# New hand-written work lists for two attention layers: alternating heads, mixed widths, and row-maximum jobs 59 ahead

## The chip, the cores and the metric

One Trainium2 chip, one of its cores, one launch. The metric is the device time of the launch in microseconds (us). Three runs of the kernel before took 1375.84, 1375.1 and 1373.46 us; their median, 1375.1 us, is the time before. Engines: PE is TensorE (matmuls), PEld its weight loads, DVE is VectorE, ACT is ScalarE, POOL is GpSimd, SP issues the DMAs.

## The reference

Two transformer layers follow each other on x of shape (4, 1024, 128), float32. Each is attention over 16 heads of 8 elements and then a gated feed-forward with 384 hidden columns; the second attention is causal. All biases and the normalisation before each part are kept.

```python
x = x + attn_a(layernorm(x))      # 16 heads of 8, softmax(q k^T / sqrt(8)) v, full
x = x + ffn(layernorm(x))         # down(silu(gate(x)) * up(x)), int weights dequantised
x = x + attn_b(layernorm(x))      # the same with a mask: key position > query position is -inf
x = x + ffn(layernorm(x))
```

## The kernel before

**Windows.** A layer's attention is 16 windows: 4 sequences times 4 groups of 4 heads. A window's queries are two halves (f = 0, 1) of 512 columns; qb counts the 128-query blocks of a half, c the four heads, kh the two halves of 512 keys. Heads 0 and 2 have their operands on partitions 0 to 63, heads 1 and 3 on 64 to 127 ("even" and "odd" heads below). In the array these are two different row groups.

**Six kinds of work, in one list.** `Plan.walk` is a list of items, and every engine runs through the same list and does its own part of each item. The string `order` gives the items of one turn (one window's worth), one letter each:

- `j`, a job: PE multiplies 128 queries by up to 512 keys (L1094) into a ring of PSUM banks (4 banks in the full layer, 3 in the causal one), and DVE takes the row maximum (L876, or L873 with the mask for a diagonal block, followed by a small read of the accumulator). 64 jobs a window in the full layer, all 512 wide; 48 in the causal one, 24 of them 512 wide (16 of these without a mask) and 8 each 384, 256 and 128 wide.
- `h`, `H`, a shift: POOL splits the negated maxima of half 0 of the next window (`h`) or half 1 of this one (`H`) into two bf16 parts (L530, L532), PE transposes them (L1144), ACT copies them (L663), and SP sends them into two rows of the query operand (L424), so that the scores come out already shifted.
- `s`, scores: PE multiplies keys by queries with the shift (L1126, one head of 512 columns in the full layer, a pair of heads in the causal one, there with four small mask matmuls at L1134 on diagonal blocks), ACT takes the exponential (L647).
- `p`, sums: PE multiplies the probabilities of four heads by v (L1160), all into bank 7.
- `N`, `n`, a norm: ACT has copied bank 7 out (L654), PE transposes it (L1022), ACT copies (L668), DVE inverts the denominators (L905), POOL scales (L540).

**Running ahead.** `jobs_ahead` says how many jobs are done before the first turn: 48 in the full layer and 44 in the causal one, that is one window less or nearly so. `sums_behind` is how many `p` items trail. PE waits at a job until DVE has emptied the bank that was used a ring ago (`ring_free`), and at scores until ACT has emptied its bank.

**Start and end.** The first 48 jobs of the full layer are done in pairs by another route (`two_pairs`, `run_pair`: PE L1071 and L1076, ACT L714, DVE L856). `SHIFT_PAIR` says before which pair the first shift's bank is awaited. 18 (PE) and 22 (DVE) jobs of the causal layer are done inside the feed-forward of the first layer (`causal_jobs`); the rest of those ahead follow once the last q and k parts are stored. SP loads a window's operands (14 DMAs, 1 MB, L387 and L390) at the `H` of the window two before; for the first two windows before the shifts.

## Time and profile before

| | |
|---|---|
| median of 3 runs | 1375.1 us (1373.46 to 1375.84) |
| profiled execution, first to last instruction | 1375.5 us |
| full layer, 14 windows in steady state (101.4 to 677.7) | 576.3 us, 41.2 us each |
| causal layer, 13 windows in steady state (909.9 to 1273.2) | 363.3 us, 27.9 us each |
| busy: PE, DVE, ACT | 1322.9, 1180.3, 1009.6 us |

The profiled span is 0.4 us above the median and inside the range of the three runs, so differences worked out from the trace can be set against the median directly. In the timeline a row is a run of equal instructions on one engine: start, duration, engine, line, operation, and in square brackets the idle time before it and what ended it. A `L1160 ... x8` row is one `p` item (four heads, two passes each). A busy PE is not PE at its peak: matmuls overlap in the records, and the start-to-start distances say more than the durations.

### The profile page before, as it was taken

What the parts mean: (1) busy time and instruction counts of PE and PEld (TensorE: products, weight loads), DVE (VectorE), ACT (ScalarE), POOL (GpSimd) and SP (SyncE); (2) the same over time, 40 slices, a digit from 0 to 9 for tenths busy, and PEclk for the clock granted to TensorE, in tenths of its full rate; (3) what the DMA queues carried; (4) which work ended last, traced back from release to release, by engine and by line L of the source; (5) the groups of instructions that cost most, each with busy time, mean ns of one, the idle gap of its engine ahead of it and who ended that gap; (6) DMA issues with size and microseconds to landing.
All of it is one profiled execution on the core that took longest, in us unless ns stands there. A gap on an engine that the chain in (4) does not pass through costs nothing.

```text
span 1375.5 us, 26857 instructions
## 1 busy us (share of the span) xinstructions
PE 1322.9 (96%) x9681; PEld 679.7 (49%) x9681; DVE 1180.3 (86%) x2979; ACT 1009.6 (73%) x1791; POOL 142.5 (10%) x309
## 2 busy tenths in 40 slices
PE   9899999999999999999988987999999999999898
PEld 6444444444444444444435764555555555555487
DVE  7799999999999999999935987788888888888376
ACT  8678888888888888888883542677677776777743
POOL 5620000000000000000001211200000000000011
PEclk9699999999999999999998997899999999999999
DMA  7611101111101111101000333121112211120001
GB/s 212 189 32 32 30 4 32 32 32 33 28 7 32 33 33 32 30 6 31 2 1 1 110 106 93 33 59 38 34 33 49 48 33 34 41 56 3 3 24 39
DMA packets 40060, 58.44 MB, mean 42 GB/s; under 512 B 7796, under 2 KB 19448, under 8 KB 39928
## 3 DMA queue, kind: packets, MB, share of 16 engines
q1 hardware_dynamic: 39928, 56.72, 17.1%
q8 instruction: 77, 1.26, 0.4%
q14 instruction: 55, 0.45, 0.1%
HBM read 36.77 MB, written 18.87 MB: 40 GB/s over the span
## 4 chain that ended last, share of the span: by engine, by line
PE 84%; DVE 6%; ACT 5%; issue 3%; POOL 1%; DMA 1%; SPq 0%; DVEq 0%; POOLq 0%; ACTq 0%
PE psum L1160 28%; PE psum L1094 24%; PE psum L1126 16%; ACT probs L647 4%; PE psum L1022 3%; PE psum L1247 3%; PE psum L1231 2%; DVE maxima L876 2%; PE psum L1134 2%; PE psum L1176 1%; PE psum L1033 1%; DVE hid L952 1%; PE psum L1071 1%; PE psum L1007 1%; DVE junk L873 1%
## 5 line engine op out<-in xcount | busy, mean ns | idle before, releaser
L647 ACT ACTIVATE probs<-psum 128x512 f32<-128x512 f32 (+3 forms) x1386 | 832.3, 666 | 218.2 <-PE psum L1126 113.5
L876 DVE TENSOR_REDUCE maxima<-psum 128x1 f32<-128x512 f32 x1232 | 773.6, 682 | 33.3 <-PE psum L1094 27.8
L1094 PE MATMUL psum<-kop,qop 62*128 62x512 f32 (+3 forms) x1744 | 562.3, 437 | 7.5 <-DVE maxima L873 1.9
L1126 PE MATMUL psum<-qop,kop 64*128 64x512 f32 (+3 forms) x1792 | 522.0, 423 | 12.8 <-ACT probs L647 5.5
L1094 PEld LDWEIGHTS psum<-kop,qop 62*128 62x128 f32 x1744 | 267.2, 188 | 378.1 <-DVE maxima L876 285.6
L1160 PE MATMUL psum<-probs,v 128*32 128x512 f32 (+3 forms) x3584 | 441.9, 565 | 0.7 <-ACT probs L647 0.5
L1126 PEld LDWEIGHTS psum<-qop,kop 64*128 64x128 f32 x1792 | 266.8, 188 | 82.6 <-ACT probs L647 45.1
L873 DVE CUSTOM_DVE_ANT_0 junk<-psum,mask 128x384 bf16<-128x384 f32 (+3 forms) x512 | 232.2, 485 | 53.0 <-PE psum L1094 51.0
L1160 PEld LDWEIGHTS psum<-probs,v 128*32 128x32 f32 x3584 | 71.1, 109 | 100.8 <-issue 69.8
L1134 PE MATMUL psum<-half_ident,key_mask 64*128 64x64 bf16 x1024 | 88.8, 197 | 0.0
L540 POOL TENSOR_TENSOR att<-att_raw,rden 128x128 f32<-128x128 f32 x64 | 26.1, 407 | 512.5 <-DVE rden L905 512.5
L530 POOL TENSOR_TENSOR shift<-negmax,zeros 128x16 bf16<-128x16 f32 x64 | 14.1, 221 | 550.1 <-DVE negmax L882 542.1
L1231 PE MATMUL psum<-ffn_xt,gate_up_w 128*128 128x512 f32 x192 | 53.9, 417 | 5.5 <-DVE hid L952 5.3
L1134 PEld LDWEIGHTS psum<-half_ident,key_mask 64*128 64x128 bf16 x1024 | 49.0, 96 | 17.9 <-issue 8.6
L1247 PE MATMUL psum<-down_w,hid 128*128 128x128 f32 x384 | 47.6, 280 | 4.9 <-DVE hid L952 4.9
L739 ACT ACTIVATE hid<-psum 128x512 f32<-128x512 f32 x48 | 28.5, 597 | 31.7 <-PE psum L1231 31.4
L905 DVE RECIPROCAL rden<-att_raw 128x16 f32<-128x16 f32 x64 | 15.7, 245 | 39.2 <-ACT att_raw L668 39.2
L1247 PEld LDWEIGHTS psum<-down_w,hid 128*128 128x128 f32 x384 | 45.0, 194 | 7.5 <-DVE hid L952 7.2
L1022 PE MATMUL psum<-ident,sums 128*128 128x128 f32 x256 | 41.1, 283 | 5.0 <-ACT sums L654 1.6
L787 DVE TENSOR_TENSOR x<-psum,x 128x512 f32<-128x512 f32 x32 | 22.1, 690 | 26.1 <-PE psum L1247 13.6
L614 ACT ACTIVATE qk<-psum,bqk 128x512 f32<-128x512 f32 x32 | 21.1, 682 | 30.2 <-PE psum L1033 30.1
L873 DVE DVE_READ_ACCUMULATOR2_ANT maxima<- 128x1 f32 x512 | 42.7, 83 | 0.1
(102 smaller groups left out, 751.6 us busy)
## 6 DMA issues: line engine op xcount, KB each, us to landing
qop<-q_parts SPq DMA_DIRECT2D x256, 64.0 KB
kop<-k_parts SPq DMA_DIRECT2D x64, 128.0 KB
kop<-k_parts SPq DMA_DIRECT2D x128, 64.0 KB
q_parts<-parts SPq DMA_DIRECT2D x24, 256.0 KB, 2.9
k_parts<-parts SPq DMA_DIRECT2D x24, 256.0 KB, 3.1
x<-in_L_attn_a_x SPq DMA_DIRECT2D x8, 256.0 KB, 4.0
q_parts<-att SPq DMA_DIRECT2D x8, 256.0 KB, 3.6
k_parts<-att SPq DMA_DIRECT2D x8, 256.0 KB, 3.6
```

The source lines that it names most:

```text
L540: nc.gpsimd.tensor_tensor(dst, att_raw[:, f, :, :, 0:HD], rden[:, f].rearrange("p t (h o) -> p t h o", o=1).broadcast_to([P, TPC, HG, HD]) ...
L647: nc.scalar.activation(probs[:, slot, heads[0] % 2:heads[-1] % 2 + 1, c0:], psum[:, bank:bank + len(heads), c0:], ACT.Exp, scale=SCORE_SCA ...
L739: nc.scalar.activation(hid[:, c, :], psum[:, 2 + 2 * (c % 2), :], ACT.Silu, scale=DEQUANT).then_inc(silu_ready, 1)
L873: nc.vector.tensor_tensor_reduce(out=junk[:, slot, 0:width], in0=src, in1=mask[:, CHUNK - width:], scale=1.0, scalar=LOWEST, op0=ALU.add, ...
L876: nc.vector.tensor_reduce(dst, src, AX_X, ALU.max).then_inc(ring_free, 1)
L1022: ins = nc.tensor.transpose(psum[:, bank, t * P:(t + 1) * P], src[:, t, :], ident[:])
L1094: mm(psum[:, bank, 0:width], qop[rows, buf, f, r, qb * P:(qb + 1) * P].bitcast(F32R), kop[rows, buf, r, kh * CHUNK:kh * CHUNK + width].bit ...
L1126: ins = mm(psum[:, bank + k, c0:], kop[rows, buf, c // 2, j * P:(j + 1) * P].bitcast(F32R), qop[rows, buf, f, c // 2, c0:].bitcast(F32R), ...
L1134: ins = mm(psum[:, bank + k, at:at + TILE_ROWS], key_mask[rows, part, :], half_ident[rows], start=False, stop=part == 1)
L1160: ins = mm(psum[32 * c:32 * c + 32, 7, c0:], v[:, at:at + 32], probs[:, slot, c % 2, c0:], start=(j == 0), stop=(s == plan.half_end[f]), t ...
L1231: ins = mm(psum[:, 2 + 2 * (c % 2) + k, :], gate_up_w[:, k, c, :].bitcast(F32R), ffn_xt[:, part].bitcast(F32R), start=part == 0, stop=part ...
L1247: ins = mm(psum[:, 7, t * P:(t + 1) * P], hid[:, c, t * P:(t + 1) * P], down_w[:, c, :], start=(c == 0), stop=(c == FB - 1))
```

## The change

Both `order` strings are replaced. The full layer's stream of jobs now alternates between an even and an odd head (`alternate=True`; the causal one did before), so the pairs of the opening stretch are numbered differently (`run_pair`) and `SHIFT_PAIR` is worked out instead of written (it becomes 22, was 20). The causal layer starts 59 jobs ahead instead of 44, which makes the walk begin one turn earlier, and its jobs come in a written list, one token `c qb kh` for each, in place of the loop's order of rising widths. All jobs, scores, sums, norms and shifts are the same ones in the same number.

```diff
@@ Plan.__init__
+        if tiles:
+            found = {x[:4]: x for x in stream}
+            stream = [found.pop((f, *(int(d) for d in token))) for f in range(2) for token in tiles[f].split()]
+            assert not found
+        self.first_job = stream[0]
@@
-        for turn in range(-1, WINDOWS + 1):
+        for turn in range(-2, WINDOWS + 1):
@@ PLANS
-PLANS = [Plan(causal=False, heads=HEAD_UNITS, unit_ring=3, job_ring=4, alternate=False,
-              order="jsjjsspjssjsjpjsjsjnsjjssp...",
+PLANS = [Plan(causal=False, heads=HEAD_UNITS, unit_ring=3, job_ring=4, alternate=True,
+              order="sjjsjpsjjjsspsjjsjspsjjsjs...",
               jobs_ahead=48, sums_behind=2, project_at=(9, 11, 14), wide_step=5),
          Plan(causal=True, heads=PAIR_UNITS, unit_ring=2, job_ring=3, alternate=True,
-              order="sjjsjpjsjsjpjjjHsjjsjpjsjjspjjsjsjsjjnjjspj...",
-              jobs_ahead=44, sums_behind=1, project_at=(4, 6, 10))]
+              order="jjHjsjjsjjjspjssjjpjsjjsjspjjssjjpsjjpjssjj...",
+              jobs_ahead=59, sums_behind=1, project_at=(4, 6, 10),
+              tiles=("120 110 030 130 020 320 330 100 230 010 220 300 000 310 210 200",
+                     "310 121 311 100 030 300 211 200 321 031 201 230 110 ..."))]
-SHIFT_PAIR = 20
+SHIFT_PAIR = 2 * -(-[item[0] for item in PLANS[0].walk].index("shift") // 4)
@@ run_pair's number; the wait for a window's operands
-                        run_pair(plan, f, c, qb, number // 2)
+                        run_pair(plan, f, c, qb, number // 4 * 2 + c % 2)
-                if (f, c, qb, kh) == (0, 0, 0, 0):
+                if job == plan.first_job:
```

Three places show how instructions move. Lines are 6 higher in the kernel after from here on (L1094 is L1100, L1126 is L1132, L1160 is L1166, L1022 is L1028, L1144 is L1150).

PE in the full layer, around the norm of half 0 of the second window (L1160 sums, L1094 jobs, L1126 scores, L1022 the norm's transposes), before:

```order
L1160 MATMUL psum<-probs,v 32x512 x4
L1094 MATMUL psum<-kop,qop 128x512
L1126 MATMUL psum<-qop,kop 128x512
L1094 MATMUL psum<-kop,qop 128x512
L1126 MATMUL psum<-qop,kop 128x512
L1094 MATMUL psum<-kop,qop 128x512
L1022 MATMUL psum<-ident,sums 128x128 x4
L1126 MATMUL psum<-qop,kop 128x512
L1094 MATMUL psum<-kop,qop 128x512 x2
```

and now, the same norm, followed by the shift of the next window:

```order
L1132 MATMUL psum<-qop,kop 128x512
L1028 MATMUL psum<-ident,sums 128x128 x4
L1150 MATMUL psum<-ident_bf,shift 32x128
L1100 MATMUL psum<-kop,qop 128x512 x2
L1132 MATMUL psum<-qop,kop 128x512
L1100 MATMUL psum<-kop,qop 128x512
L1132 MATMUL psum<-qop,kop 128x512 x2
L1166 MATMUL psum<-probs,v 32x512 x4
L1132 MATMUL psum<-qop,kop 128x512 x2
L1100 MATMUL psum<-kop,qop 128x512 x3
```

The norm stood three jobs behind the last `p` of its half; four more `p` items now lie between, and the shift `h` follows it at once, with 6 jobs from there to the scores that use it (11 before).

PE at the start of the causal layer, from the first shift (L1144) to the first scores (L1126), before:

```order
L1144 MATMUL psum<-ident_bf,shift 32x128
L1094 MATMUL psum<-kop,qop 128x512 x2
L1094 MATMUL psum<-kop,qop 128x384 x2
L1094 MATMUL psum<-kop,qop 128x512 x4
L1126 MATMUL psum<-qop,kop 128x512 x2
```

and now, with both shifts of the first window ahead of its scores:

```order
L1150 MATMUL psum<-ident_bf,shift 32x128
L1100 MATMUL psum<-kop,qop 128x384 x2
L1100 MATMUL psum<-kop,qop 128x512
L1100 MATMUL psum<-kop,qop 128x128
L1100 MATMUL psum<-kop,qop 128x512
L1100 MATMUL psum<-kop,qop 128x256
L1100 MATMUL psum<-kop,qop 128x384
L1100 MATMUL psum<-kop,qop 128x128 x2
L1150 MATMUL psum<-ident_bf,shift 32x128
L1100 MATMUL psum<-kop,qop 128x256
L1132 MATMUL psum<-qop,kop 128x512 x2
```

44 jobs stood ahead of the first scores, 62 do now; the first shift is transposed after job 52 (was 36), the second after job 61.

PE in the causal layer's steady state, around its two norms, now (before they stood apart, 17 jobs from each other; L1140 is the mask):

```order
L1166 MATMUL psum<-probs,v 32x512 x4
L1100 MATMUL psum<-kop,qop 128x256
L1100 MATMUL psum<-kop,qop 128x512 x2
L1150 MATMUL psum<-ident_bf,shift 32x128
L1028 MATMUL psum<-ident,sums 128x128 x8
L1100 MATMUL psum<-kop,qop 128x384 x2
L1132 MATMUL psum<-qop,kop 128x256 x2
L1140 MATMUL psum<-half_ident,key_mask 128x64 x4
L1100 MATMUL psum<-kop,qop 128x512
L1166 MATMUL psum<-probs,v 32x384 x4
```

A shift and both norms now stand in one block, and jobs of 256, 512 and 384 columns stand next to each other.

## Rows read from the trace of the kernel before

**Rows 1.** The page, part 1: busy us, share of the span, instructions.
```profile
PE 1322.9 (96%) x9681; PEld 679.7 (49%) x9681; DVE 1180.3 (86%) x2979; ACT 1009.6 (73%) x1791; POOL 142.5 (10%) x309
```
**Rows 2.** Busy us by stretch: length, PE, PEld, DVE, ACT, POOL, then granted clock.
```profile
101.40:677.70 576.30, 572.30 (x3726) 241.92 (x3725) 560.69 (x953) 485.60 (x981) 23.12 (x84) 1.00 0.12 26
852.10:873.70 21.60, 21.16 (x128) 11.78 (x128) 13.06 (x49) 11.99 (x16) 9.74 (x5) 0.51 0.23 50
909.90:1273.20 363.30, 359.62 (x3460) 190.19 (x3462) 315.22 (x1092) 264.14 (x391) 21.43 (x78) 1.00 0.18 37
```
**Rows 3.** Who waited for whom, 101.4 to 677.7 us: total, times, longest.
```profile
PEld psum L1094 <- DVE maxima L876: 209.7, 308, 0.8
...
DVE maxima L876 <- PE psum L1094: 10.5, 28, 0.4
```
**Rows 4.** Timeline of a full-layer window: PE between two sums.
```profile
304.04 1.07 PE L1160 MATMUL psum<-probs,v 128*32 128x512 f32 x8
305.04 0.49 PE L1094 MATMUL psum<-kop,qop 62*128 62x512 f32 x1
...
305.94 0.64 PE L1160 MATMUL psum<-probs,v 128*32 128x512 f32 x4
```
**Rows 5.** The same window: DVE's jobs, and PE and DVE around its norm.
```profile
304.34 15.12 DVE L876 TENSOR_REDUCE maxima<-psum 128x1 f32<-128x512 f32 x24
...
318.07 0.42 PEld L1022 LDWEIGHTS psum<-ident,sums 128*128 128x128 f32 x4 [0.51 <-issue]
...
321.13 0.69 DVE L876 TENSOR_REDUCE maxima<-psum 128x1 f32<-128x512 f32 x1 [0.38 <-PE psum L1094]
```
**Rows 6.** PE at the last shift and the scores that need it.
```profile
1282.29 0.22 PE L1144 MATMUL psum<-ident_bf,shift 128*32 128x128 bf16 x1 [0.17 <-POOL shift L532]
...
1285.43 0.78 PE L1126 MATMUL psum<-qop,kop 64*128 64x512 f32 x4 [0.28 <-DMA qop<-shift_rows]
```
**Rows 7.** Who waited for whom, 909.9 to 1273.2 us.
```profile
DVE junk L873 <- PE psum L1094: 38.6, 103, 0.7
...
DVE maxima L876 <- PE psum L1094: 7.6, 13, 0.6
```
**Rows 8.** DVE in a causal window: masked jobs of 512 and 128 columns.
```profile
1056.26 0.68 DVE L873 CUSTOM_DVE_ANT_0 junk<-psum,mask 128x512 bf16<-128x512 f32 x1
...
1056.87 0.69 DVE L873 CUSTOM_DVE_ANT_0 junk<-psum,mask 128x512 bf16<-128x512 f32 x1
...
1058.80 0.29 DVE L873 CUSTOM_DVE_ANT_0 junk<-psum,mask 128x128 bf16<-128x128 f32 x1 [0.72 <-PE psum L1094]
```
**Rows 9.** Causal layer: sums on PE, exponentials of two heads on ACT.
```profile
1033.72 0.64 PE L1160 MATMUL psum<-probs,v 128*32 128x256 f32 x8
...
1035.10 2.85 ACT L647 ACTIVATE probs<-psum 128x1024 f32<-128x1024 f32 x3 [0.26 <-PE psum L1126]
...
1038.52 0.85 PE L1160 MATMUL psum<-probs,v 128*32 128x384 f32 x8
...
1040.43 1.06 PE L1160 MATMUL psum<-probs,v 128*32 128x512 f32 x8
...
1042.60 1.07 PE L1160 MATMUL psum<-probs,v 128*32 128x512 f32 x8
```
**Rows 10.** The start of the causal layer.
```profile
847.08 1.38 SPq L424 DMA_DIRECT2D qop<-shift_rows  x2
...
848.65 0.69 DVE L873 CUSTOM_DVE_ANT_0 junk<-psum,mask 128x512 bf16<-128x512 f32 x1
...
852.08 0.79 PE L1126 MATMUL psum<-qop,kop 64*128 64x512 f32 x2 [3.71 <-DMA qop<-shift_rows]
...
853.63 1.29 DVE L876 TENSOR_REDUCE maxima<-psum 128x1 f32<-128x512 f32 x2 [4.29 <-PE psum L1094]
```
**Rows 11.** PE at the first scores of the second and of the last causal window.
```profile
886.68 0.48 PE L1126 MATMUL psum<-qop,kop 64*128 64x512 f32 x2
...
1277.76 0.48 PE L1126 MATMUL psum<-qop,kop 64*128 64x512 f32 x2
```

More of the change, by code:

```diff
@@ L51, with __init__ @@
 class Plan:
-    def __init__(self, causal, heads, unit_ring, job_ring, alternate, order, jobs_ahead, sums_behind, project_at, wide_step=99):
+    def __init__(self, causal, heads, unit_ring, job_ring, alternate, order, jobs_ahead, sums_behind, project_at, wide_step=99, tiles=None):
         self.causal, self.heads, self.unit_ring, self.job_ring = causal, heads, unit_ring, job_ring
@@ L82, in __init__ @@
                 width = (TPC * f + qb + 1) * P if causal else S
-                tiles = [(c, kh) for r in range(PAIRS) for kh in range(2) for c in (2 * r, 2 * r + 1)] if alternate \
+                in_head_order = [(c, kh) for r in range(PAIRS) for kh in range(2) for c in (2 * r, 2 * r + 1)] if alternate \
                     else [(c, kh) for c in range(HG) for kh in range(2)]
-                for c, kh in tiles:
+                for c, kh in in_head_order:
                     w = min(width - kh * CHUNK, CHUNK)
@@ L147 @@
 PAIR_UNITS, HEAD_UNITS = ((0, 1), (2, 3)), ((0,), (1,), (2,), (3,))
-PLANS = [Plan(causal=False, heads=HEAD_UNITS, unit_ring=3, job_ring=4, alternate=False,
-              order="jsjjsspjssjsjpjsjsjnsjjsspjssjsjpjsjsjsjjsspjssjsjpHjsjsjsjjsspjssjsjpjsjsjsjjsspjssjsjpjsjsjNsjjsspjssjsjpjsjsjsjjsspjssjsjphjsjsjsjjsspjssjsjpjsjs",
+PLANS = [Plan(causal=False, heads=HEAD_UNITS, unit_ring=3, job_ring=4, alternate=True,
+              order="sjjsjpsjjjsspsjjsjspsjjsjspsjsjsjjsjssjjsjspHssjjsjpsjjsjspjjsjsspjsjssjsjjsnjsjjsspjssjsjpjssjsjpjssjsjpsjjsjspsjjsjspsjjsjsjsjsjsNhjjsjsspssjjjsps",
               jobs_ahead=48, sums_behind=2, project_at=(9, 11, 14), wide_step=5),
          Plan(causal=True, heads=PAIR_UNITS, unit_ring=2, job_ring=3, alternate=True,
-              order="sjjsjpjsjsjpjjjHsjjsjpjsjjspjjsjsjsjjnjjspjsjsjjpjsjjsjpjjsjsjpjjsjNjjsphjjspjjjspjjspjs",
-              jobs_ahead=44, sums_behind=1, project_at=(4, 6, 10))]
-SHIFT_PAIR = 20
-assert [item[0] for item in PLANS[0].walk].index("shift") in range(2 * SHIFT_PAIR - 3, 2 * SHIFT_PAIR + 1)
+              order="jjHjsjjsjjjspjssjjpjsjjsjspjjssjjpsjjpjssjjpjsjjsjpsjjjspjjssjjpjjsjspjjjhnNjjsjpjjssjjp",
+              jobs_ahead=59, sums_behind=1, project_at=(4, 6, 10),
+              tiles=("120 110 030 130 020 320 330 100 230 010 220 300 000 310 210 200",
+                     "310 121 311 100 030 300 211 200 321 031 201 230 110 231 120 210 221 330 021 001 320 010 301 331 111 000 101 011 131 220 130 020"))]
+SHIFT_PAIR = 2 * -(-[item[0] for item in PLANS[0].walk].index("shift") // 4)
 PE_JOBS_AHEAD, DVE_JOBS_AHEAD = 18, 22
```

## The prediction

> **What bounds the kernel now.** The page comes first: PE is busy for 96% of the span and DVE for 86% [rows 1]. An average over unlike stages says little, so I split the span by stretches [rows 2]. In the 14 steady windows of the full layer DVE works 560.69 of 576.3 us: 15.6 us idle, 1.1 a window. In the 13 steady windows of the causal layer it works 315.22 of 363.3: 48.1 us idle, 3.7 a window. The waits say who keeps DVE idle: PE, for 10.5 us in 28 waits (two a window) in the full layer [rows 3] and 46.2 us in 116 waits in the causal one [rows 7]. PE waits for DVE as well, 209.7 us by its weight loads in the full layer [rows 3], much of it while the sums before still stream. The full layer is thus DVE's, with a small hole at each norm; the causal layer belongs to neither, PE and DVE take turns.
>
> That caps the gain. No list can take more than 1.1 us from a full window, as DVE's jobs stay the same: 24 of them take 15.12 us, 0.63 apiece [rows 5], and 64 x 0.63 is 40.3 of the window's 41.2.
>
> **The full layer's list: PE's share.** Rows 4 give PE's prices: sums begin at 304.04, the next work at 305.04, the next sums at 305.94. So sums cost 1.00, and the six matmuls between 0.90. At the granted clock of 1.00 [rows 2], 2.4 GHz, 512 columns take 0.213, so six in a row would be 1.28: some run side by side. An even and an odd head lie on different rows of the array. The six are (o odd, e even; j job, s scores) jo so se je so je; if only unequal parities overlap, that makes four turns (jo; so with se; je with so; je) of 0.225 each. Counted by the list, a window had 80 such turns; the new list has 64, the least possible for 128 matmuls in pairs. PE gets 16 x 0.225 = 3.6 us lighter a window. Before it had about 16 x 1.0 + 80 x 0.225 + 2 norms and 2 shifts (2) = 36 of 41.2 us, now 32.4.
>
> The Trainium skill ("TensorE: Matmul & The Clock Gate", Part 3, the mechanism) says that a weight load overlaps running matmuls only when its row group differs. By it the six matmuls need four turns, 0.85 us, and the trace's 0.90 agrees [rows 4]; with three turns, as if any two overlapped, they would need 0.64, and the new list would then save PE nothing.
>
> This work lies beside DVE's, so it buys only the holes. The hole: the norm's transposes come three jobs behind the last sums and need ACT's copy of them; PE's weight load stands idle 0.51 us until 318.07, and DVE idles 0.38 before its next job at 321.13 [rows 5]. Now four more sums lie between the last sum of a half and its norm, so that wait goes, at both norms: 28 waits, 10.5 us in 14 windows, 0.75 each. What comes new: stretches with four scores around one sum between two jobs (s s p s s): two turns and the sums, 0.45 + 1.00 us of PE, while a ring of four jobs feeds DVE for 2.5 us, less the 0.5 from a matmul's start to its reduce; and the shift H only 4 jobs behind the last job of its half, where POOL's result comes about 0.1 us after PE does. I let these cost 0.2. A window gains 0.53, 15 windows 8 us. Bounds: 0 and the whole idle time, 16.
>
> The shift h stands 6 jobs before the scores that need it, 11 before. From the transpose to the landing took 3.14 us in the one place where scores waited for it, 1282.29 to 1285.43 [rows 6]. Six jobs are 3.8 us, and seven scores lie there too. It fits with 0.6 to spare; I count nothing, and 0.5 a window if ACT is late with the copy. The first window's shift is 4 jobs later (job 42, was 38) with one pair of pairs behind it: +0.4. In the tail three sums instead of two stand behind the last scores: +0.5.
>
> **The causal layer: steady state.** I cut a window at its sums and add up for each stretch what each engine must do. Prices: DVE 0.61, 0.48, 0.35 and 0.22 for a masked job of 512, 384, 256, 128 columns (starts at 1056.26 and 1056.87; the durations 0.69 and 0.29 at 512 and 128 columns give 0.13 for each 128 [rows 8]), 0.63 unmasked; PE 1.00 for sums of 512 columns [rows 4] 0.225 a turn of 512, narrower in proportion, and as estimates 0.43 for sums of 128 (those between in line), 0.2 for a mask's four, 0.75 a norm, 0.3 a shift; ACT 0.95 for a pair of heads at 512 (2.85 for three [rows 9]), in proportion below. For example the stretch from 1033.72 to 1038.52 took 4.80 us [rows 9]: DVE 4.70, PE 3.2, ACT 4.0, so it was DVE's. The ones from 1038.52 and 1040.43 took 1.91 and 2.17: DVE 1.70 and 1.83, PE 1.8 and 1.9, so PE's or nobody's. Over twelve stretches the largest of the three sums to 26.8 before and 27.8 was measured; the new list sums to 26.9, its PE work to 24.7 (24.4 before) and DVE's to the same 24.0. PE's is larger since the written list puts three odd heads in a row (310 121 311): 47.4 turns, 45.9 before.
>
> So without carrying over, nothing is won. The lists differ in what can be carried: before one stretch has 1.5 us more DVE than PE work, and then eight have less, and behind sums the queue of three jobs often holds 128 or 256 columns, 0.2 to 0.4 us of cover against 1.0 of sums: there DVE idles, as 0.72 before 1058.80 [rows 8]. With mixed widths no stretch has more than 0.6 excess, which three queued jobs of mean 0.5 can carry. Of the 1.5 us of excesses I take a third as saved: 0.5 a window, 14 windows, 7 us. Bounds: 1.9 gained (half of DVE's idle time) and 0.8 lost (PE's 0.3 and 0.5 at the block of h and both norms, where PE is away from jobs for 0.3 + 2 x 0.75 = 1.8 us and the queue holds 1.2 to 1.5).
>
> **The causal layer: start and end.** DVE had its 44 jobs done at 849.3 and stood still until 853.63, since the first shift's DMA went out only at 847.08, behind the operands' 14, and landed at 852.08 [rows 10]. Now 59 jobs must be emptied before PE reaches the first scores. By the prices above jobs 0 to 58 are 28.8 us of DVE, jobs 0 to 43 were 21.0: 7.8 more; the first job of window 1 may wait 0.5 for its operands, which land just ahead of that 852.08. Scores begin at 857.8, 5.7 later. The 4.3 us hole is filled by that. Given back: the granted clock was 0.51, the 1.2 GHz level, from 852.1 to 873.7 [rows 2], and the turn from 852.08 to 886.68 took 34.6 instead of 27.9 [rows 10, 11]: 6.7 us over 21.6 at the low level; if the clock returns at the same moment, 5.7 of these pass without scores, -1.7. At the end turn 14 has 14 jobs fewer and PE's 23.4 bounds it, about 24.5: -3.4; the last turn from 1277.76 [rows 11] loses its 4 jobs: -0.5. Sum +0.1. In the feed-forward, the first nine causal jobs are wide now (4.45 us of DVE, was 2.76), of which 0.4 shows.
>
> Operands: load of window w+2 now waits for the last sums of w-1, 29 jobs or 16 us before their first use; The shift that queued behind such a load landed 5 us after its issue at 847.08 [rows 10]; with 0.6 for each of a load's 14 issues (an estimate from that row's 1.38 for two) a load is in after some 8.4 + 5 = 13 us. Hidden by 3; were it not, 1 us a window. SP has nothing else queued behind that wait but the next shift, 33 jobs later.
>
> **Sum.** -8.0 + 0.4 + 0.5 - 7.0 + 0.1 + 0.4 = -13.6. The profiled execution (span 1375.5) is 0.4 above the median of 1375.1, so the sum is set against the median: 1361.5 us.
>
> **Rivals.** (a) The mixed widths do more: DVE's idle time in the causal layer halves, 1.9 a window, 27 us; with the full layer's 8 it gives 1341. For it: 103 of its waits come from masked jobs [rows 7], which the list spreads. Against: PE's own work is 24.7 of 27.9. (b) Slower: the causal list makes PE the bound. Same-parity jobs (0.3) and the block h n N with two waiting inverses on DVE (0.5, or up to 1.2 together with idle DVE behind it) cost 1.2 x 14 = 17, the later start its 5.7 with 1.5 given back; with 8 gained in the full layer: 1375.1 + 17 + 4.2 - 8 = 1388 at worst, 1380 at 0.6 a window. It decides when PE's work per window passes what the balance saves, about 0.4 us. (c) Nothing changes: holes at the norms in the full layer reappear at the tight places (s s p s s, H four jobs behind), and the causal layer comes out even: 1374.5. For it: DVE is at 97% there already, and the two lists' stretch sums differ by 0.1.
>
> **Chances.** The forecast, 1350 to 1371: 0.50. (a) 0.15. (b) 0.22. (c) 0.13, of which 0.02 ends just beyond what can be told. A measurement of this kernel tells about 0.2%, 2.7 us, from no change. From these: faster 0.50 + 0.15 + 0.02 = 0.67, same 0.11, slower 0.22. The range reaches to (a) and into (b): 1341 to 1382; the forecast's own is 1350 to 1371.
>
> **What would show it.** Full layer: a window of 40.7, waits of DVE for PE under 4 us in 14 windows, PE's weight loads waiting longer for DVE than before; wrong if scores wait for the shift's DMA in each window. Causal layer: a steady window of 27.4, DVE idle near 3.2, fewer waits after narrow jobs; wrong with DVE idle above 4 or a window above 28. Start: the causal layer's first scores near 852.1 - 6.7 + 5.7 = 851, and no 4.3 us hole of DVE ahead of them. End: about 4 us shorter from the first scores of window 14. The forecast fails as a whole if the full layer is not faster, since its gain rests on the removed wait alone.

## The result and the profile after

The changed kernel took 1335.1 us (median of 4 runs, 1332.8 to 1338.3) against 1374.6 for the kernel before in the same comparison: ratio 0.972, 95% interval 0.970 to 0.974. That is 39.5 us less; 13.6 were forecast and the range ended at 1341. The profiled execution has a span of 1336.4 us (1375.5 before). Here and below medians and ranges take in every execution, while a ratio leaves out those that ran over 1.5% above the fastest of their kernel, which is so in one run, the causal order alone (two of its four).

By milestones of the two traces, in us:

| stretch | before | after | difference | predicted |
|---|---|---|---|---|
| to the first scores of the full layer | 64.7 | 66.2 | +1.6 | +0.4 |
| first to last scores, full layer | 662.2 | 637.8 | -24.3 | -8.0 |
| from there to the first causal job | 91.5 | 89.4 | -2.1 | +0.5 |
| to the first causal scores | 33.8 | 44.0 | +10.3 | +6.1 |
| first to last scores, causal layer | 455.6 | 432.1 | -23.5 | -12.6 |
| to the end | 67.8 | 66.9 | -0.9 | 0 |

The last column sorts the prediction's terms into these stretches; in the causal one it is -7.0, -1.7, -3.4 and -0.5.

Busy us by stretch of the changed kernel (length, PE, PE's weight loads, DVE, ACT, POOL, granted clock, then DMA): ten full windows, ten causal ones, and the causal turn 14.

```profile
199.73:594.23 394.50, 392.32 (x2662) 158.14 (x2663) 393.63 (x681) 347.46 (x701) 17.01 (x60) 1.00 0.14 29
951.09:1219.50 268.41, 268.16 (x2661) 144.88 (x2661) 246.36 (x841) 199.79 (x300) 16.16 (x60) 1.00 0.19 42
1219.50:1243.90 24.40, 24.28 (x255) 13.00 (x255) 19.57 (x62) 19.98 (x30) 1.61 (x6) 1.00 0.01 3
```

The same cut of the kernel before, ten windows each, so that windows can be compared one to one (they are in line with [rows 2]):

```profile
204.33:616.00 411.67, 408.83 (x2662) 172.79 (x2661) 400.51 (x681) 346.84 (x702) 16.51 (x60) 1.00 0.13 27
975.36:1254.90 279.54, 276.56 (x2662) 146.32 (x2662) 242.48 (x841) 203.18 (x300) 16.49 (x60) 1.00 0.19 40
```

A full window fell from 41.17 to 39.45 us, a causal one from 27.95 to 26.84. The first is the surprise: the prediction had called 40.3 the least that any list could reach. DVE's *busy* time fell as well, from 40.05 to 39.36 a window, with the very same 681 instructions in ten windows. It is idle for 0.09 us a window now, where it was for 1.12. So of the 1.72 us that a window lost, 1.03 came out of DVE's idle time and 0.69 out of its busy time. In the causal layer DVE's idle time went from 3.7 to 2.2 a window, while its busy time rose from 24.2 to 24.6.

Who waits for whom in the same ten full windows after. Against [rows 3] PE's wait for DVE before a job has shrunk, its wait for ACT before scores has taken over, and DVE's wait for PE is gone from the list (in ten windows before they were 149.8, 6.7 and 7.5 us):

```profile
PEld psum L1132 <- ACT probs L653: 105.5, 170, 0.8
PEld psum L1100 <- DVE maxima L882: 46.3, 70, 0.8
```

The start of the causal layer after, which answers to [rows 10]: DVE waits while PE projects, PE waits for window 1's operands, and the first scores come at 837.47, 44.0 us behind the first causal job.

```profile
811.54 0.89 DVE L804 TENSOR_TENSOR v<-psum,bvo 128x128 f32<-128x128 f32 x4 [2.40 <-PE psum L1041]
...
830.39 0.87 PE L1100 MATMUL psum<-kop,qop 62*128 62x384 f32 x3 [1.38 <-DMA kop<-k_parts]
...
831.24 0.56 DVE L879 CUSTOM_DVE_ANT_0 junk<-psum,mask 128x384 bf16<-128x384 f32 x1 [1.26 <-PE psum L1100]
...
837.47 1.00 PE L1132 MATMUL psum<-qop,kop 64*128 64x512 f32 x2
```

### The profile page after: what moved, and what is told of

Read it like the earlier page. It is cut to its first block, busy times and chain, and to the rows that moved or that the text cites. A ratio compares the mean times of both kernels' runs of the same rounds, so it can differ in the third digit from the quotient of the medians.

```text
span 1336.4 us, 26857 instructions
## 1 busy us (share of the span) xinstructions
PE 1290.7 (97%) x9681; PEld 656.2 (49%) x9681; DVE 1176.7 (88%) x2979; ACT 1004.5 (75%) x1791; POOL 142.1 (11%) x309
## 3 DMA queue, kind: packets, MB, share of 16 engines
q8 instruction: 77, 1.26, 0.4%
## 4 chain that ended last, share of the span: by engine, by line
PE 88%; DVE 5%; ACT 3%; issue 2%; DMA 1%; SPq 0%; POOL 0%; DVEq 0%; ACTq 0%; POOLq 0%
PE psum L1166 30%; PE psum L1132 21%; PE psum L1100 21%; PE psum L1253 4%; PE psum L1028 3%; PE psum L1237 2%; ACT probs L653 2%; PE psum L1140 2%; PE psum L1039 1%; DVE maxima L882 1%; DVE hid L958 1%; PE psum L1182 1%; PE psum L1077 1%; PE psum L1013 1%; PE psum L1150 1%
## 5 line engine op out<-in xcount | busy, mean ns | idle before, releaser
L653 ACT ACTIVATE probs<-psum 128x512 f32<-128x512 f32 (+3 forms) x1386 | 821.8, 669 | 153.0 <-PE psum L1132 83.0
L1100 PE MATMUL psum<-kop,qop 62*128 62x512 f32 (+2 forms) x1744 | 519.4, 429 | 7.0 <-DVE maxima L879 3.1
L1132 PE MATMUL psum<-qop,kop 64*128 64x512 f32 (+3 forms) x1792 | 514.2, 427 | 9.2 <-ACT probs L653 7.9
L1166 PE MATMUL psum<-probs,v 128*32 128x512 f32 (+3 forms) x3584 | 440.5, 564 | 0.7 <-ACT sums L660 0.7
L1100 PEld LDWEIGHTS psum<-kop,qop 62*128 62x128 f32 x1744 | 266.4, 189 | 203.4 <-DVE maxima L882 119.3
L1132 PEld LDWEIGHTS psum<-qop,kop 64*128 64x128 f32 x1792 | 247.5, 187 | 232.1 <-ACT probs L653 205.9
L879 DVE CUSTOM_DVE_ANT_0 junk<-psum,mask 128x512 bf16<-128x512 f32 (+3 forms) x512 | 232.6, 487 | 38.7 <-PE psum L1100 34.9
L1166 PEld LDWEIGHTS psum<-probs,v 128*32 128x32 f32 x3584 | 71.1, 108 | 120.0 <-issue 89.2
L1140 PE MATMUL psum<-half_ident,key_mask 64*128 64x64 bf16 x1024 | 74.3, 197 | 0.0
L669 ACT CAST shift_rows<-psum 32x128 f32<-32x128 bf16 x64 | 16.5, 258 | 56.2 <-PE psum L1150 56.2
L1140 PEld LDWEIGHTS psum<-half_ident,key_mask 64*128 64x128 bf16 x1024 | 43.2, 96 | 18.4 <-issue 6.5
L745 ACT ACTIVATE hid<-psum 128x512 f32<-128x512 f32 x48 | 28.5, 598 | 30.3 <-PE psum L1237 29.9
L620 ACT ACTIVATE qk<-psum,bqk 128x512 f32<-128x512 f32 x32 | 21.1, 684 | 32.8 <-PE psum L1039 32.6
L1028 PE MATMUL psum<-ident,sums 128*128 128x128 f32 x256 | 38.7, 283 | 2.4 <-ACT sums L660 1.6
```

The costliest lines, as they stand in the source:

```text
L653: nc.scalar.activation(probs[:, slot, heads[0] % 2:heads[-1] % 2 + 1, c0:], psum[:, bank:bank + len(heads), c0:], ACT.Exp, scale=SCORE_SCA ...
L745: nc.scalar.activation(hid[:, c, :], psum[:, 2 + 2 * (c % 2), :], ACT.Silu, scale=DEQUANT).then_inc(silu_ready, 1)
L879: nc.vector.tensor_tensor_reduce(out=junk[:, slot, 0:width], in0=src, in1=mask[:, CHUNK - width:], scale=1.0, scalar=LOWEST, op0=ALU.add, ...
L1028: ins = nc.tensor.transpose(psum[:, bank, t * P:(t + 1) * P], src[:, t, :], ident[:])
L1100: mm(psum[:, bank, 0:width], qop[rows, buf, f, r, qb * P:(qb + 1) * P].bitcast(F32R), kop[rows, buf, r, kh * CHUNK:kh * CHUNK + width].bit ...
L1132: ins = mm(psum[:, bank + k, c0:], kop[rows, buf, c // 2, j * P:(j + 1) * P].bitcast(F32R), qop[rows, buf, f, c // 2, c0:].bitcast(F32R), ...
```

## The experiments

"Window" is the mean of ten in the profiled execution, cut at ACT's copies of the shift. A run without a ratio is a single execution. The kernel before stood at 1374.9 to 1376.9 us in the comparisons with several rounds, at 1374.1 in the last.

### Which list gives what

The first run takes the new full list and leaves the causal layer as it was.

```diff
 # the changed kernel, but PLANS[1] as before
-order="jjHjsjjsjjjspjss...", jobs_ahead=59, ..., tiles=("120 110 ...", "310 121 ..."))]
+order="sjjsjpjsjsjpjjjH...", jobs_ahead=44, ...)]
```

> The full layer wholly new, the causal layer wholly old. If the two layers' gains add up: full window 39.4 as in the kernel after, causal window 27.9 as before, first causal scores 28.7 us behind the last addition of the first feed-forward's chunk as before, the whole at 1375 - 24 - 2 = 1349. If the causal lists are what shortens the start or the clock's stretches elsewhere, it lies outside 1345 to 1353.

Measured: 1352.4 us, ratio 0.983 (0.981 to 0.985). The full window is 39.45, the causal one 27.96. So the full list brings 23 us, and the causal one the other 17 (1352.4 to 1335.1): each layer's window is the same whichever list the other layer has, and both gains are larger than forecast.

### The two parts of the full list, one at a time

```diff
 # heads alone: the old order of letters, but
-Plan(..., alternate=False,
+Plan(..., alternate=True,
```

> The kernel before with only the heads of the full layer's jobs alternating; both orders, the 44 jobs ahead and the causal widths are the old ones. Theory A (the alternation of heads relieves PE: 80 turns of 512 columns become fewer, DVE's jobs are no longer a little late): a full window falls from 41.2 to about 39.8 us, the whole to about 1355. Theory B (the order of the letters does it, where the sums stand between jobs; parity is worth little): a full window stays within 0.3 of 41.2, the whole within 5 us of 1375.

```diff
 # order alone: alternate=False, but
-order="jsjjsspjssjsjpjsjsjnsjjssp...",
+order="sjjsjpsjjjsspsjjsjspsjjsjs...",
```

> The full layer gets the new order but its jobs keep the old sequence of heads (two halves of keys of one head after each other); the causal layer is the old one. Theory A (heads): a full window near 41, the whole near 1373. Theory B (order): a full window of 39.4 to 39.8, the whole about 1350. If it takes both, it lies above 41.2 here, as the order was drawn up for pairs that this kernel does not have.

Measured: heads alone 1417.2 us, ratio 1.031 (1.029 to 1.034), window 44.1. Order alone 1389.4, ratio 1.010 (1.008 to 1.012), window 41.9. Each part alone makes the kernel slower, by 41 and by 14 us; together they save 23. The two were written for each other: the order says which kinds of matmul are neighbours, the sequence of heads says which of these lie on different rows of the array.

PE with the heads alone, between two sums; this is the stretch of [rows 4], which had 0.90 us between the end of one sums' 1.00 and the start of the next:

```profile
309.56 0.50 PE L1098 MATMUL psum<-kop,qop 62*128 62x512 f32 x1
309.57 0.72 PE L1130 MATMUL psum<-qop,kop 64*128 64x512 f32 x2
309.91 0.40 PE L1098 MATMUL psum<-kop,qop 62*128 62x512 f32 x1
310.14 0.39 PE L1130 MATMUL psum<-qop,kop 64*128 64x512 f32 x1
310.37 0.40 PE L1098 MATMUL psum<-kop,qop 62*128 62x512 f32 x1
310.70 1.06 PE L1164 MATMUL psum<-probs,v 128*32 128x512 f32 x8
```

The six matmuls take 1.13 us instead of 0.90: the last score and the last job are both of odd heads now, and start 0.23 apart (310.14 and 310.37). In the kernel before they start together (310.68 and 310.69), and the next sums follow at 311.01:

```profile
310.10 0.49 PE L1094 MATMUL psum<-kop,qop 62*128 62x512 f32 x1
310.11 0.73 PE L1126 MATMUL psum<-qop,kop 64*128 64x512 f32 x2
310.45 0.40 PE L1094 MATMUL psum<-kop,qop 62*128 62x512 f32 x1
310.68 0.39 PE L1126 MATMUL psum<-qop,kop 64*128 64x512 f32 x1
310.69 0.39 PE L1094 MATMUL psum<-kop,qop 62*128 62x512 f32 x1
```

DVE with the heads alone: three jobs, and then it waits for PE.

```profile
310.10 1.89 DVE L880 TENSOR_REDUCE maxima<-psum 128x1 f32<-128x512 f32 x3 [0.25 <-PE psum L1098]
312.23 1.89 DVE L880 TENSOR_REDUCE maxima<-psum 128x1 f32<-128x512 f32 x3 [0.24 <-PE psum L1098]
```

### Where the rest of the full window went

The traces of before and after differ in something that no row calls a wait. A fed DVE starts its jobs of 512 columns 0.600 to 0.610 us apart, while one lasts 0.68 in the records: it overlaps the next by 0.08. A job that starts less than 0.08 late shows no idle time. In the kernel before, 44 of the 60 distances a window between neighbouring jobs are at most 0.61, but some 14 are 0.63 to 0.74 (the other two are the holes at the norms); after, 52 are at most 0.61, and 8 are 0.63 to 0.73. Four runs ask who makes them late.

```diff
 # lighter sums, odd key blocks only (their results are left out but for 64 columns; 1.0 is added)
-mm(psum[..., c0:], v[...], probs[..., c0:], ...)
+mm(psum[..., c0:end], v[...], probs[..., c0:end], ...)     # end = c0 + 64 if j % 2 == 1
```

> The kernel before with PE made lighter: the sums of odd key blocks cover 64 columns instead of up to 512 (these sums are left out beyond that, and 1.0 is added to every sum to keep the denominators away from zero). DVE's jobs are untouched. Theory: DVE's jobs cost 0.605 from start to start and not the 0.63 of the prediction; the rest was lateness of PE of under 0.1 a job that shows as no idle time because a job's recorded end overlaps the next start. Then a full window falls from 41.2 to 39.4, and mean start-to-start distances from 0.638 to about 0.608. Rival: 0.63 is DVE's own pace in that list (PSUM banks shared with ACT and PE): the full window stays at 40.5 or more. In the causal layer a window of 24.5 to 26 would say that PE bounds it, 27 or more that it does not.

Measured: 1359.6 us, window 40.30, between the theory's 39.4 and the rival's 40.5. Nearly the whole of the lateness is gone but for four distances a window at the norms, and PE is idle for 1.9 us a window where it was idle for 0.3.

```diff
 # the last job of each long stretch one score later, 8 times a window
-...jjssp...
+...jsjsp...
```

> The kernel before; in its full layer the last job of every long stretch goes one score later, next to the sums (jsjjssp becomes jsjsjsp, 8 times a window), nothing else. In the trace of before about 13 of 64 jobs a window start 0.07 to 0.13 us late on DVE without any idle time that the rows show. Theory 1, they are late because two scores and the sums lie between two jobs there: the distance between those jobs falls by a score's 0.23, the lateness goes, the window falls from 41.2 to about 40.3 us, the time by 13. Theory 2, the place of the sums is set by ACT, which frees the scores' three banks, and the job only moves within the same time: the window stays at 41.1 to 41.3.

Measured: 1372.0 us, window 41.31. Theory 2. The place of that job is free: what moved is only which matmul waits. PE's scores waited for ACT 40 times in ten windows before (6.7 us), and in this run, ten windows:

```profile
PEld psum L1126 <- ACT probs L647: 38.5, 160, 0.4
```

```diff
 # both norms two sums later, at the same place of the next long stretch
-...jsjsjnsjjssp...      ...jsjsjNsjjssp...
+...jsjsjsjjssp (jssjsj p) jsjsjnsjjssp...
```

> The kernel before with both norms of the full layer two sums later, at the same place of the next long stretch (after the third of its five jobs), nothing else. The prediction's theory, a norm's hole comes from its wait for ACT's copy of the last sums: that wait goes, 0.5 to 0.75 us a window, 40.5 us and 8 to 10 us of the time. Rival, the hole is the 0.75 us of transposes themselves, in a stretch where PE has no time to spare, wherever they stand: 41.1 to 41.4.

Measured: 1375.6 us, window 41.34. Moving the norm away from the last sums of its half, which the prediction called the gain of the new list, brings nothing: DVE still waits for PE twice a window (7.8 us in 25 waits between 125 and 640 us, 9.3 in 25 before).

```diff
 # ACT: exponentials of odd key blocks over 256 of 512 columns, full layer
-nc.scalar.activation(probs[..., c0:], psum[..., c0:], ACT.Exp, ...)
+nc.scalar.activation(probs[..., c0:end], psum[..., c0:end], ACT.Exp, ...)     # end = 256
```

> The kernel before, but in the full layer ACT's exponentials of odd key blocks cover only 256 of 512 columns (the rest of those blocks is left as it was): 32 of 64 a window are 0.2 us shorter, 6.8 us of ACT's 34 a window; PE's and DVE's work stays. Theory A, in the old list the five scores between two jobs' sums wait for ACT to free the three banks, and that sets when the sums and the next jobs come: the window falls from 41.2 to 40.0 to 40.6 us. Theory B, PE and DVE alone set it: 41.1 to 41.2.

Measured: 1352.2 us, window 39.70, more than theory A had asked for. With the old list, and neither PE's nor DVE's work touched, 1.5 of the 1.7 us are there. DVE still waits for PE twice a window, 4.1 us in ten.

So the old window was set by a circle that has no DVE in it. The rows of the kernel before, ACT's exponentials, PE's scores (L1126) and its sums (L1160):

```profile
307.54 2.56 ACT L647 ACTIVATE probs<-psum 128x512 f32<-128x512 f32 x5
308.59 0.58 PE L1126 MATMUL psum<-qop,kop 64*128 64x512 f32 x2
309.11 1.07 PE L1160 MATMUL psum<-probs,v 128*32 128x512 f32 x8
310.11 0.73 PE L1126 MATMUL psum<-qop,kop 64*128 64x512 f32 x2
310.87 0.60 ACT L647 ACTIVATE probs<-psum 128x512 f32<-128x512 f32 x1 [0.77 <-PE psum L1126]
...
311.01 1.07 PE L1160 MATMUL psum<-probs,v 128*32 128x512 f32 x8
312.01 0.50 PE L1126 MATMUL psum<-qop,kop 64*128 64x512 f32 x1
```

Follow it round. The scores have a ring of three banks, so the fifth score of a long stretch needs the end of its second exponential. ACT begins the five at 307.54 and is at the end of the second some 1.1 us later; the fifth score starts just then (the second of the two in the row at 308.59). The sums stand behind it, 309.11; the next scores behind the sums, 310.11; ACT has been idle for 0.77 by then. Then the short stretch, sums at 311.01, the first score of the next long stretch at 312.01, its exponential 0.57 later: 312.58, that is 5.04 us after 307.54. DVE needs 8 x 0.605 = 4.84 for the eight jobs of this time. From sums to sums, the eight rounds of a window take 5.03 four times, 5.07 twice (with a shift) and 5.46 twice (with a norm's transposes), which is the window's 41.2. With the shorter exponentials the round of 5.03 takes 4.84, DVE's own time. Each of the four runs fits: a shorter exponential or shorter sums shorten the circle, a moved job or norm does not.

After, PE and ACT go in even steps of 1.90 for thirteen of a window's sixteen sums, mostly three scores and three jobs between two sums:

```profile
302.86 1.06 PE L1166 MATMUL psum<-probs,v 128*32 128x512 f32 x8
...
304.75 1.07 PE L1166 MATMUL psum<-probs,v 128*32 128x512 f32 x8
...
306.65 0.64 PE L1166 MATMUL psum<-probs,v 128*32 128x512 f32 x4
```

The scores that are left over stand in three long stretches of eight or nine (4.6, 4.8 and 5.4 us between their sums). In a step of 1.90 PE works all the time, 1.00 + 0.90, and DVE needs 3 x 0.605 = 1.82 for its three jobs: this is where some are a little late still.

The same relief of PE on the changed kernel shows what is left:

```diff
 # the changed kernel with the lighter sums of the first run of this section
```

> The changed kernel with the weighted sums of odd key blocks cut to 64 columns, as in the run on the kernel before (a stand-in is added so that nothing divides by zero): some 0.8 us less of PE at every second sums. Theory 1, the full layer is DVE's now, and its queue never runs dry: the full window stays at 39.4 us, 0.9 below what the old list reached with the same relief (40.3). Causal layer: if PE ends last there, its window falls from 26.8 to 26.0 or less, if DVE and ACT, it stays above 26.5. Theory 2, PE still sets the full window: 38.9 or less.

Measured: 1334.1 us in all, hardly less than the changed kernel's 1335.1, as the clock was low in one full and two steady causal windows (0.87, 0.74 and 0.88 granted; the two causal ones took 32.6 and 29.3 us). The full window is 38.77, most of the other causal windows 26.5. Ten full windows:

```profile
197.97:585.69 387.72, 382.46 (x2662) 172.61 (x2662) 387.71 (x681) 344.94 (x700) 16.90 (x60) 1.00 0.14 29
```

Neither theory: it is between them. DVE is busy for 387.71 of 387.72, its jobs 0.598 apart. This is DVE's real floor, 38.8; the changed kernel is 0.7 above it, in the eight late starts a window that no row calls a wait.

### The two parts of the causal list

```diff
 # order alone: the changed kernel without the written widths
-              tiles=("120 110 030 130 ...", "310 121 311 100 ..."))]
+              tiles=None)]
```

> The changed kernel, but the causal layer takes its jobs in the loop's sequence of widths; its new order of letters and the 59 jobs ahead stay. Counted by the list, PE's jobs and scores between two sums need 41.5 turns a window (the larger count of even or odd heads in each stretch), against 45.8 in the changed kernel and 42.0 before. Theory W, the mixed widths carry the causal gain: the window goes back to 27.9 us and the time to 1350 us. Theory O, the order of letters carries it: the window stays at 26.9 and the time at 1335, a little lower for the lighter PE. Theory P, order and widths are written for each other, as order and heads were in the full layer: the window is above 28.3 and the time above 1356.

```diff
 # widths alone: the changed kernel with the old causal order and 44 ahead
-order="jjHjsjjsjjjspjss...", jobs_ahead=59,
+order="sjjsjpjsjsjpjjjH...", jobs_ahead=44,
```

> The changed kernel, but the causal layer has its old order of letters and 44 jobs ahead; only the written list of widths is new there. 46.2 turns a window. Theory W: the window is 26.9 us and, with the old start, the time 1333 to 1338. Theory O: the window goes back to 27.9 and the time to 1350 or more. Theory P: the window is above 28.3 and the time above 1356.

Measured: 1403.6 us (1380 to 1410), ratio 1.010 (1.002 to 1.018), and 1402.0 (1392 to 1406), ratio 1.020 (1.018 to 1.023). Theory P. With the order alone, two causal windows at the full clock and one with a low clock:

```profile
1055.90:1084.80 28.90, 28.38 (x271) 14.26 (x267) 24.67 (x85) 20.48 (x30) 1.59 (x7) 1.00 0.18 39
1187.00:1216.00 29.00, 28.46 (x274) 14.45 (x266) 24.78 (x85) 20.52 (x31) 1.66 (x8) 1.00 0.19 39
...
1247.40:1281.50 34.10, 33.58 (x268) 17.06 (x268) 24.93 (x85) 20.82 (x30) 1.61 (x6) 0.80 0.16 33
```

With the widths alone, one of each:

```profile
1010.30:1040.20 29.90, 28.67 (x268) 14.93 (x268) 24.62 (x84) 20.24 (x30) 1.65 (x6) 1.00 0.18 37
1040.20:1073.90 33.70, 32.66 (x268) 16.98 (x270) 24.86 (x84) 20.74 (x31) 1.65 (x6) 0.85 0.15 34
```

At the full clock a window is 28.9 with the order alone and 29.9 with the widths alone; both lists old give 27.96, both new 26.84. It is the picture of the full layer again: each part spoils what the other half was tuned to. On top, the granted clock fell to the 1.2 GHz level inside steady causal windows, in more than half of them for the order alone and in three for the widths alone (in the profiled executions, of 1408 and 1392 us); such a window costs another 4 to 5 us. So the windows bear Theory P out, while the times hold the clock's share too: 0.9 and 2.0 us a window over the old causal list are some 13 and 28 us in fourteen windows (an estimate), of the 51 and 50 us that these runs took over the one with that list. PE was idle for 0.5 and 1.2 us of a window at the full clock there, for 0.3 in the kernel before and 0.03 in the changed one.

### Even and odd heads in the causal list

```diff
 # 16 of 48 tokens, only the head (first digit) changes, widths stay; the first ones:
-"120 110 030 130 020 320 330 100 230 010 220 300 000 310 210 200"
+"120 110 230 030 020 320 330 100 130 010 220 000 300 210 310 200"
```

> The changed kernel with the same widths in the same places of the causal list; only which head a job is of is exchanged between jobs of equal width, at 16 of 48 places, so that in each stretch between sums even and odd heads are near equal: 42.25 turns a window instead of 45.75, that is 3.5 x 0.225 = 0.8 us less of PE's work. DVE's and ACT's work stays as it is, in length and order. Theory 1, PE ends last in a causal window: 0.4 to 0.8 a window less, 14 windows: 1324 to 1330 us. Theory 2, DVE and ACT bound the window, DVE with 2.2 us of idle time that the scores' waits for ACT leave: nothing within 3 us of 1335.

Measured: 1344.6 us, ratio 0.978 (0.976 to 0.979), window 27.32: 0.5 slower than the changed kernel, against both theories. Stretch by stretch, the three whose count fell most, by 0.75 to 1 turn, kept their time within 0.08 us (2.74 and 2.73, 2.03 and 2.05, 3.25 and 3.33), and two got longer. One of them in the changed kernel, its last two jobs and the next sums:

```profile
1064.47 0.42 PE L1166 MATMUL psum<-probs,v 128*32 128x128 f32 x8
...
1065.83 0.40 PE L1100 MATMUL psum<-kop,qop 62*128 62x512 f32 x2
1066.16 0.42 PE L1166 MATMUL psum<-probs,v 128*32 128x256 f32 x4
```

and with the exchanged heads:

```profile
1068.35 0.42 PE L1166 MATMUL psum<-probs,v 128*32 128x128 f32 x8
...
1069.76 0.64 PE L1100 MATMUL psum<-kop,qop 62*128 62x512 f32 x2
1070.32 0.42 PE L1166 MATMUL psum<-probs,v 128*32 128x256 f32 x4
```

An even and an odd job start together (the pair lasts 0.40) and the sums follow 0.33 behind; two odd ones start one behind the other (0.64) and the sums follow after 0.56. The stretch grew from 1.69 to 1.97, the other one, with two even jobs at its end, from 1.52 to 1.73: together the 0.5.

```diff
 # 6 of 48 tokens; the two stretches above as in the changed kernel
-"... 020 320 330 100 230 010 220 300 000 310 210 200", "310 121 311 100 030 300 211 200 ..."
+"... 020 220 330 100 230 310 320 300 000 010 210 200", "310 121 211 100 030 300 311 200 ..."
```

> The changed kernel with heads exchanged at six of 48 places of the causal list, between jobs of equal width: 42.75 turns a window by the same count as in the run with balanced heads, 45.75 in the changed kernel. That run's list made two stretches longer, by 0.2 and 0.3 us, where its two last jobs before the sums came to be of one parity; these two stretches are kept here as in the changed kernel. Theory 1, only the last matmuls ahead of the sums count, those that follow PE's last wait in the stretch, and turns saved elsewhere lie beside PE's waits for DVE and ACT: the window stays at 26.8 us and the time within 3 us of 1335. Theory 2, turns count wherever they lie: 42.75 turns give 26.1 us and 1325. Theory 3, what made the other list slower was something else, as the 16 exchanges: 27.1 or more, 1340.

Measured: 1334.7 us, ratio 0.970 (0.967 to 0.973), window 26.88. Theory 1. A count of 42.75 turns and one of 45.75 take the same time; what tells is the pair that stands last before the sums. It is also not clearly better than the changed kernel (0.972, 0.970 to 0.974), so no version here beats it.

### Does the causal layer wait for ACT?

```diff
 # causal layer: exponentials of every second step over the first half of their columns
+end = (c0 + CHUNK) // 2 if plan.causal and s % 2 == 1 else CHUNK
```

> The kernel before, but in the causal layer ACT's exponentials of every second step cover only the first half of their columns (the rest is left as it was, and a stand-in is added to the sums so that nothing divides by zero): 12 of 24 a window are shorter, by 1.9 us of ACT's 20.3 in all. PE's and DVE's work stays. Theory A, the old causal list is held by scores that wait for ACT, as the old full list was: its window falls from 27.9 to 27.3 us or less. Theory B, it is held by PE's and DVE's turns: 27.7 to 27.9.

> The same relief on the changed kernel. Theory A: if the new list still waits for ACT, its window falls from 26.8 to 26.4 us or less; if the new list has taken ACT out of what bounds the window, it stays at 26.7 to 26.8. Theory B: 26.7 to 26.8 with the old list unchanged as well.

Measured: 1376.2 us with the old lists, window 28.03; 1334.7 with the new ones, window 26.77. ACT's busy time fell by 3 us a window in both (2.9 and 2.8; 1.9 were expected) and nothing followed. So ACT does not hold the causal window, in either list. Theory B's other half, that PE's and DVE's turns do, is not shown: the lighter sums, which shorten PE's, moved the causal windows by 0.4 in the old list (27.54, where 27 or more was to say that PE does not bound it) and by 0.3 in the new one (26.5). What holds a causal window, and what in the new list gives the 1.11, no run isolates. What the traces show is that DVE's waits for PE before masked jobs fell from 80 to 50 in ten windows, and those before unmasked ones (5.9 us in 10 waits) are gone. The first row is of the ten windows before, the second of the ten after:

```profile
DVE junk L873 <- PE psum L1094: 30.4, 80, 0.7
...
DVE junk L879 <- PE psum L1100: 18.9, 50, 0.8
```

## Why the prediction was wrong

Faster was right; the size was not. One of the signs to look for in the full layer came, DVE's waits for PE are gone. Another came out the other way: PE's weight loads were to wait longer for DVE, and they wait for 46.3 us in ten windows instead of 149.8. And moving the norms, the reason given for the full layer's gain, brings nothing by itself; that this layer got faster all the same was luck. Point by point:

**"The full layer is thus DVE's, with a small hole at each norm"; "no list can take more than 1.1 us from a full window".** This is the step that failed. It rests on 24 jobs in 15.12 us, 0.63 apiece [rows 5]. But 0.63 was not a price. The 24 hold late starts, up to 0.08 us of each hidden as busy time by the records' overlap; fed, a job costs 0.605, and with nothing in the way 0.598. The floor was 38.8, not 40.3, and the list took 1.72 of 41.17, not 0.53: 1.03 of idle time, nearly all that the prediction allowed for, and 0.69 of busy time, which it took as fixed. From the first to the last scores that is 24.3 us, of which 8 were forecast. The bound at the other end, 16, was too low for the same reason.

**"So it buys only the holes"; the norm's wait.** The waits of DVE for PE did vanish [rows 3], as predicted, but they were a result and not the cause: with the norms moved away in the old list, nothing is gained. The cause was the circle of ACT's exponentials, the three banks and two sums, 5.03 us for eight jobs that need 4.84; the shorter exponentials, with nothing else changed, gave 1.46 of the 1.72. The prediction had all its rows before it and read only DVE's waits. It never added up what one round of scores, exponential and sums takes.

**Turns: "a window had 80 such turns; the new list has 64".** Wrong, and without effect on the sum only since it was held to be hidden. The rows of the six matmuls (310.10 to 310.69, in the section on the two parts of the full list) show three starts, two matmuls each, not four, and 0.90 is one first turn of 0.335, one of 0.235 and 0.33 to the sums; that four turns of 0.213 come near it was chance. Counting in each stretch the larger of its even and odd heads gives 64 before (66 if a norm parts its stretch), 80 for the heads alone, 70 (74) for the order alone, 64 after, which puts the four windows of 41.2, 44.1, 41.9 and 39.4 in their order. By this count PE's share was the same in both lists. The Trainium skill ("TensorE: Matmul & The Clock Gate", Part 3, the mechanism) says that matmuls keep the program's order in start and end; the rows with the heads alone agree (309.56 to 310.37, in order). Read as strict pairing in that order, this gives four turns for both sequences of six, and the trace has 0.90 for one and 1.13 for the other. The count by the larger share is not exact either, as the causal layer's 42.75 against 45.75 shows; the exact rule stays open.

**Start and tail of the full layer, +0.4 and +0.5.** The first scores came 1.6 later; from the last ones to the causal layer's first job it took 2.1 less, for which I have no cause but the clock: in this stretch it was low for 6.8 us before (from 736.8) and not at all now.

**Causal steady state, -0.5 a window.** The mechanism named, narrow jobs that leave DVE uncovered behind sums, agrees with DVE's idle time, 3.7 before and 2.2 now, with its fewer waits before masked jobs and with the two runs that rule ACT out; no run tests it by itself. The term was too small by half: 1.11 a window, 14.4 us in the thirteen steady ones, where "a third" of the 1.5 us of excess was taken as saved; 1.11 would be three quarters. Rival (a) had taken 1.9 for it. Rival (b), a slower window with PE as the bound through odd heads in a row, did not come: the window is shorter, and three turns fewer (26.88) change nothing.

**The clock given back, -1.7.** The first causal window took 34.6 us before and 33.2 now. The clock was low for 21.2 us of it and now for 16.7, but the window is 6.4 above the steady 26.84, and was 6.7 above 27.95: of the 1.7, only 0.3 came.

**Turn 14, -3.4.** Confirmed: 24.40 us in the row above, 27.8 before.

**The start, +5.7 and +0.4.** Measured +10.3. Of the time from the first causal job to the last one ahead of the scores, 44.1 us now and 31.0 before, DVE works 37.0 and 28.4: 8.6 more, where 7.8 and 0.4 were predicted. But it is idle for 7.1 instead of 2.6: 2.40 once at 811.54, where its jobs in the feed-forward run out before PE's projection, 1.26 at the operands of window 1, which the prediction had at 0.5, 1.17 and 0.60 at 798.4 and 800.6, both waiting for PE, and the rest in waits of less than 0.4. Less the hole of 2.8 that is filled, this is 10.3.

**The end.** From the first scores of window 15 to the last ones it took 30.0 us before [rows 11] and takes 25.7 now (1243.89 to 1269.55); 0.5 was forecast. Gone from it are, besides the four jobs, the last shift with its wait for the DMA (0.8 us of PE's weight load), one of twelve sums, which now comes after the last scores, and 3.4 us at a clock of 0.5 (from 1289.8 before, none now). The prediction counted the jobs alone; how much each of the others is worth, no run tells.

## What to carry to other kernels

When three engines hand work to each other through rings of a few banks, add up each closed circle (matmul, exponential, bank free, sums, next matmul) beside each engine's own work; an engine that is busy for 97% may still be the one that is led. Compare start-to-start distances with the shortest one seen before calling a mean duration a price. An order and what it orders are one thing: judge a new list only as a whole, since here each half alone made it slower, by 41 and 14 us in the full layer and by 0.9 and 2.0 us a window at the full clock in the causal one, and the halves together saved 23 and 17 us.

## What the runs showed of the hardware

A DVE reduce of 512 columns is recorded with 0.68 us and repeats every 0.598 to 0.610; up to 0.08 us of waiting a job is thus booked as work (40.05 us of busy time a window before, 39.36 after, for the same instructions). Two jobs of one parity right ahead of the sums cost 0.2 to 0.3 us more than an even and an odd one; exchanges of heads at other places of the list changed the window by 0.04 us (26.84 and 26.88). And the granted clock fell to 0.5 for a time inside steady causal windows of the two half-new lists (PE idle for 0.5 us of 28.9 and 1.2 of 29.9) and in two of the changed kernel with lighter sums (0.8 of 26.8), but never in the ten full windows with lighter sums before, where PE was idle for 1.9 us of 40.3. Nor does the longest idle stretch of PE tell them apart: 0.48 us with the widths alone, where the clock fell, 0.66 with the lighter sums before, where it did not. What decides it is left open.
